# Turning a chunk's normalised rows last in its step, in the first 4-head layer of a four-block attention kernel

## What is computed

```python
def _layer_norm(x, g, b):
    mean = jnp.mean(x, axis=-1, keepdims=True)
    std = jnp.std(x, axis=-1, keepdims=True, ddof=1)
    return g * (x - mean) / (std + EPS) + b
def _mha_layer(q, k, v, Wq, bq, Wk, bk, Wv, bv, gamma, beta):
    ...
    attn = jax.nn.softmax(scores, axis=-1)
    ...
    out = jnp.einsum('hbqk,hbkd->hbqd', attn, Vh)
    out = out.transpose(1, 2, 0, 3).reshape(B, Sq, d)
    out = out + q
    return _layer_norm(out, gamma, beta)
...
for i in range(L):
    enc = _mha_layer(q, k, v, Wq[i], bq[i], Wk[i], bk[i], Wv[i], bv[i], gamma[i], beta[i])
    enc = jax.nn.leaky_relu(enc @ Wff[i] + bff[i], negative_slope=0.2) + enc
    q, k, v = (enc, enc, enc)
```

## Time and profile before

| | us |
|---|---|
| median of 3 runs (lowest, highest) | 1656.14 (1652.9, 1657.09) |
| the profiled execution | 1650.79 |
| its span | 1649.0 |
| PE busy | 1377.1 (84%) |
| DVE busy | 1053.1 (64%) |
| ACT busy | 757.9 (46%) |
| POOL busy | 523.9 (32%) |

### The profile page before, as it was taken

One profiled execution on the slowest core, in us unless ns is written; L12 is line 12 of the kernel. 1 busy time (PEld: TensorE's weight loads), 2 busy tenths in 40 slices (PEclk: granted clock), 3 DMA queues, 4 the chain that ended last, 5 costly groups with the idle time before them and its releaser, 6 DMA issues.

```text
span 1649.0 us, 22006 instructions
## 1 busy us (share of the span) xinstructions
PE 1377.1 (84%) x7498; PEld 795.2 (48%) x7498; DVE 1053.1 (64%) x2640; ACT 757.9 (46%) x1062; POOL 523.9 (32%) x330
## 2 busy tenths in 40 slices
PE   5878999999759978788999869799997668588896
PEld 3423333333348856543444346444443557444796
DVE  5677777777265357756566458676563877675754
ACT  5304555555767444532333435233334534254664
POOL 4000000000231033215777842178876436101222
PEclk8958999999969999998999979799997889899998
DMA  6853333330000000364312306713400020640001
GB/s 233 218 143 55 55 55 55 56 55 2 26 1 1 1 1 32 115 198 90 87 44 52 106 1 185 206 44 90 91 26 26 1 33 1 155 81 3 1 1 51
DMA packets 79850, 110.32 MB, mean 67 GB/s; under 512 B 16576, under 2 KB 55674, under 8 KB 77946
## 3 DMA queue, kind: packets, MB, share of 16 engines
q1 hardware_dynamic: 79737, 108.91, 26.6%
HBM read 70.55 MB, written 37.80 MB: 66 GB/s over the span
## 4 chain that ended last, share of the span: by engine, by line
PE 36%; DVE 22%; POOLq 19%; issue 9%; ACT 6%; DVEq 3%; DMA 2%; POOL 1%; SPq 1%; ACTq 0%
POOLq L1057 19%; PE banks L1145 5%; PE banks L1459 5%; PE banks L1444 4%; PE banks L1088 4%; PE banks L2007 3%; PE banks L1121 3%; DVE max_parts L1282 3%; DVE mask_rows L1278 2%; DVE scratch L1278 2%; PE banks L1099 1%; PE banks L2033 1%; PE banks L2023 1%; DVE max_parts L1267 1%; ACT x_feat L1245 1%
## 5 line engine op out<-in xcount | busy, mean ns | idle before, releaser
L1245 ACT ACTIVATE x_feat<-banks,key_bias 128x1024 f32<-128x1024 f32 x160 | 176.4, 1113 | 271.6 <-PE banks L1130 210.2
L1056 POOL TENSOR_TENSOR x_feat<-x_feat 128x1024 f32<-128x1024 f32 x112 | 269.3, 2405 | 75.1 <-ACT x_feat L1245 63.2
L1088 PE MATMUL banks<-stacks 128*128 128x512 f32 (+4 forms) x640 | 229.2, 405 | 30.0 <-DVE max_parts L1271 9.2
L1145 PE MATMUL banks<-x_feat,v_group 128*64 128x512 f32 (+4 forms) x1312 | 232.1, 568 | 10.9 <-ACT x_feat L1245 10.3
L1245 ACT ACTIVATE x_feat<-banks 128x1024 f32<-128x1024 f32 (+3 forms) x224 | 179.5, 839 | 125.5 <-PE banks L1124 84.5
L1088 PEld LDWEIGHTS banks<-stacks 96*128 96x128 bf16 (+1 forms) x640 | 77.4, 138 | 200.0 <-DVE max_parts L1271 87.8
L1414 POOL TENSOR_TENSOR stacks<-w_even,stacks 128x512 fp32r<-128x512 f32 x16 | 21.9, 1396 | 463.1 <-ACT stacks L1406 463.1
L1121 PE MATMUL banks<-stacks 99*128 99x512 bf16 (+3 forms) x512 | 139.5, 347 | 11.4 <-DMA stacks<-neg_max_parts 6.7
L1271 DVE CUSTOM_DVE_ANT_0 scratch<-banks,mask_rows 128x512 f32<-128x512 f32 x128 | 88.2, 689 | 54.6 <-PE banks L1088 54.6
L1129 PE MATMUL banks<-stacks 128*128 128x512 f32 x256 | 111.2, 434 | 9.5 <-DMA stacks<-neg_max_parts_r 9.5
L1444 PE MATMUL banks<-stacks 128*128 128x512 f32 x384 | 102.5, 406 | 8.2 <-DVE stacks L1426 4.0
(11 more groups left out here) (286 smaller groups left out, 2570.3 us busy)
## 6 DMA issues: line engine op xcount, KB each, us to landing
stacks<-q_parts_r SPq DMA_DIRECT2D x18, 512.0 KB, 12.2
stacks<-k_parts_r SPq DMA_DIRECT2D x18, 512.0 KB, 14.2
q_parts_r<-stacks SPq DMA_DIRECT2D x16, 512.0 KB, 2.8
k_parts_r<-stacks SPq DMA_DIRECT2D x16, 512.0 KB, 3.6
v_group<-v SPq DMA_DIRECT2D x14, 512.0 KB, 14.7
stacks<-q_parts SPq DMA_DIRECT2D x16, 384.0 KB, 5.2
w_even<-in_w SPq DMA_DIRECT2D x4, 1024.0 KB, 6.7
stacks<-q_parts SPq DMA_DIRECT2D x16, 256.0 KB, 5.4
```

Of the source, the lines that this page charges most:

```text
L1056: e.tensor_tensor(total, total, p, ALU.add)
L1088: m = e.matmul(PS[:, bank, at:at + wide], q[0:rows, h, qt * P:(qt + 1) * P], keys[0:rows, h, k0:k0 + wide], start=True, stop=True, skip_gr ...
L1145: m = e.matmul(PS[w * h:w * (h + 1), bank, t.q0:CH], V[:, h, :], PB[:, t.index % 2, h // 2, h % 2, 0:CH - t.q0], start=t.first, stop=t.las ...
L1245: e.activation(dst, PS[:, 2 * (st % 2):2 * (st % 2) + 2, 0:CH - t.q0], ACT.Exp, scale=A.scale, bias=bias).then_inc(s.p_ready, 1)
```

## The change

In the first layer alone (`front`), three things move. On PE, the turn of `y_tok` goes from behind the scores to the end of step i = 2. On PE again, the first half of the feed-forward goes in step i = 3 from ahead of the mask's turn and of `turn_weights` to behind them. On ACT, the copies of the turned `y_tok` go from the head of step i = 2 to its end.

```diff
@@ layer_tensor
-            if i == 2 and ok(-1):
+            if i == 2 and not front and ok(-1):
                 e.wait_ge(nm.normed, c)
                 turn("y", c - 1, Y3)
-            if i == 3 and ok(-1):
+            if i == 3 and not front and ok(-1):
                 forward(c - 1, 0)
...
             if front and 0 < t <= NT:
                 turn_weights(t - 1)
+            if i == 3 and front and ok(-1):
+                forward(c - 1, 0)
...
             if front and 0 < t <= NT:
                 with_values(t - 1)
+            if i == 2 and front and ok(-1):
+                e.wait_ge(nm.normed, c)
+                turn("y", c - 1, Y3)
@@ layer_scalar
-            if i == 2 and ok(-1):
+            if i == 2 and not front and ok(-1):
                 take("y", c - 1, (COLS["gamma"] + 2 * l, COLS["beta"] + 2 * l))
...
             if i > 1 and ok(-2):
                 take_projected(c - 2, i - 2)
+            if i == 2 and front and ok(-1):
+                take("y", c - 1, (COLS["gamma"] + 2 * l, COLS["beta"] + 2 * l))
```

## The result

The changed kernel took 1642.91 us (median of 8 runs, 1636.98 to 1649.01) against 1655.49 us before (8 runs). The ratio is 0.9927, with a 95% interval of 0.9902 to 0.9953: faster by 12.1 us, interval 7.8 to 16.2. Timed again later beside other kernels, the same kernel gave 0.9954 (0.9931 to 0.9977). The 9.8 us forecast lie in both intervals. Taken off the median that the forecast started from, the first ratio gives 1656.14 x 0.9927 = 1644.0, at the fast end of the range of 1643 to 1652.

The account below looks back on a forecast made before the run. No engine is full; PE waits 14.2 us in four chunks of the first 4-head layer for normalised rows. Filling them gives 1.9 + 3.3 + 2.7 + 1.9 = 9.8 us off 1656.14: 1646.3, range 1643 to 1652.

Parts of the forecast that it names:

- Chunk 0: First 512 tokens of the first 4-head layer: scores of tile 7 start earlier, gain 1.9 us, 1.0 at half clock.
- Chunk 1: Second 512 tokens: feed-forward starts at 644.0 instead of 647.30, gain 3.3 us, 2.1 with the half clock left.
- The 1.6 us of clock: Chunk 1's eight query and projection matmuls: 1.6 us come back if the half clock came from the wait before.
- Chunk 2: Third 512 tokens: scores of tile 15 start at 676.3 instead of 679.00, gain 2.7 us, bounds 2.1 and 3.1.
- Chunk 3: Last 512 tokens, no scores left: feed-forward starts at 706.1 instead of 708.04, gain 1.9 us, bounds 1.7 and 2.1.
- Behind 708 us the stage is PE and DVE back to back and shifts whole: From chunk 3's feed-forward to the stage's end: everything moves earlier together, so the gain is not hidden.
- B: PE waits instead for ACT's weights copy, 2.2 us behind the normalise: only 4.8 us gained, 1651.3; chance 0.14.
- C: Stage's end: the next attention's loads land no earlier and are waited for, gain given back, 1656; chance 0.05.
- D: Slower: `y` turned and copied later delays the mask's turn and feed-forward, 1662 with 1.5 us each; chance 0.05.
- the prediction's estimate of 7.5 us: Sum if a table-load drain preceded each weights copy: about 2.3 us lower, 1.4 at chunk 0, 0.9 at chunk 2.

Follow-up runs that it names:

- the run with chunks 0 to 2: The change applied to chunks 0 to 2 only, chunk 3 keeping the old order: stage 165.41 us against 170.54 before, ratio 0.9941.
- the small matmuls in the kernel before: Kernel before, order untouched, with 52, 30, 60 and 76 unused constant matmuls ahead of the `y_tok` turns: stage 166.81 us against 170.54, ratio 0.9966.
- the second trace: The changed kernel run once more, unaltered: stage 161.76 us against 162.72 in the first trace, ratio to before 0.9954.
- turn only: Against before, only the turn of `y_tok` and its copies move, the feed-forward keeping its old place: stage 164.30 us, ratio 0.9966.
- beta late: The change, with DVE adding beta behind subtraction and value in chunk 3: stage 159.37 us against the change's 162.72, ratio to before 0.9945.
- the small matmuls in chunk 3 alone: The change plus 24, 10 and 40 unused constant matmuls in chunk 3's PE waits: stage 160.83 us against the change's 162.72, ratio to before 0.9904.

## Why the prediction came out right, step by step

**The sum.** 9.8 us forecast, 7.8 and 8.8 in two traces of the stage (8.8 and 9.0 by the chunks), 12.1 (7.8 to 16.2) and 7.6 (3.8 to 11.4) in the times. Mechanism and sign were right, the single terms were not all. In part the nearness of the sum is luck: 1.3 us that the forecast priced at nothing (the feed-forward's own move) stand against 1.4 to 2.6 us that chunk 3 did not give.

**Chunk 0,** 1.9 forecast: 1.80 and 1.81. Where the stage's first 32 us differ (32.81 against 31.80), a half clock met other matmuls ahead of the change's first instruction.

**Chunk 1,** 3.3 forecast: 4.12 and 3.07. The 1.6 us of clock came back in one trace and partly in the other, in the run with chunks 0 to 2 not at all. That the half clock came from the wait before it is borne out by the small matmuls in the kernel before: 3.60 us in place of 5.19. It may not be the only wait that does it: in the second trace and in the run with chunks 0 to 2 the matmuls met a half clock with no wait for `y_tok` ahead of them, in a stretch that begins within 2 us of the 2.54 us that PE waits for GpSimd's weights in step 9. The feed-forward's start came 3.5 us earlier against the normalise (7.65, before 11.18), forecast 3.3; the rest of 4.12 is its own move.

**Chunk 2,** 2.7 forecast: 3.57 in both. The scores of tile 15 start 2.7 us earlier against the normalise, as said (671.18 - 664.94 = 6.24, before 679.00 - 670.04 = 8.96), and 3.0 in the second trace, at full clock, where the forecast had 3.1. The missing term is the feed-forward's own move, which the forecast priced at nothing: with the turn in place it fills PE's waits of 0.88 and 0.57 us for the value bank, worth 0.74 in chunk 2 and 0.59 in chunk 1 (turn only against the change).

**Chunk 3,** 1.9 forecast: -0.66 and +0.51. Here a step failed. The feed-forward does start 1.8 us earlier against the normalise (7.03 us, before 8.86), by the very chain forecast: ACT's early copy, DVE's wait for GpSimd, beta, subtraction, value. But "Behind 708 us the stage is PE and DVE back to back and shifts whole" left out that PE has less to do in front of it and sits idle for 2.5 us, behind which the feed-forward and projection run at half clock: 2.7 us more for these two in the first trace, 1.6 in the second. With small matmuls in the waits this loss is gone, with beta late the loss and part of the wait. The term itself was also too large: the 1.8 us hold against a kernel before whose turn and projection ran in part at half clock (1.97 and 2.46 us in chunk 3); with small matmuls in the waits of both orders the new one is 0.7 us ahead.

**The rivals.** B (the wait moves to ACT) holds in chunk 0, as the forecast had it, and in part in chunk 2 once the clock is full: 1.12 us ahead of L2059 in the second trace. C (given back at the end) did not come: from the second half of chunk 3's feed-forward to the row DMAs it takes 33.95 us before (714.51 to 748.46) and 33.95 with the change (706.50 to 740.45). D did not come: the feed-forward waits for the copies of `y_tok` nowhere in the change, 0.4 us in one chunk if only the turn is moved; the mask's turn waits for them once, 0.7 us in chunk 3 of the second trace, where PE then waits for DVE anyway. The drain that the Trainium skill, page "ScalarE: Activation LUTs", section "What ACT_TABLE_LOAD costs", adds to a table load is not in these traces either (the exponential starts 613.93 - 612.64 - 1.28 = 0.01 us behind it), so the prediction's estimate of 7.5 us from that page has no support here, near as it is to the first stage's 7.8.

**Order and clock apart.** Before with its waits filled by matmuls that compute nothing: -3.7 us, the clock's part. The change then adds the order's: in chunks 0 to 2, 25.95 + 32.59 + 28.49 = 87.03 against 79.97, 7.1 us. That the throttled state is the default and activity releases it is what the Trainium skill, page "TensorE: Matmul & The Clock Gate", section "What's actually happening", states; the run of before with small matmuls agrees (mean granted clock of the stage 0.95 against 0.90).

**What stays open.** The first timing of the change shows 4 us more than its stage, the second 1 us less; over the twelve timed kernels the ratios show on average some 2 us more gain than the stages and 1 us more than the chunks, the small matmuls in chunk 3 alone 6 and 4. Whether the later stages, which no edit touches, gain a little or the draws were lucky can't be told: their length ranges from 896.9 to 914.4 us in these traces.

## What to carry to other kernels

Where one queue serves a pipeline of steps, put the instruction that waits for the longest chain last in its step, and check on each other engine that its partner (here ACT's copies) moves too, else the order deadlocks (by the code; it was not run) or the exponential's chain stays behind it. Count what really lies between old and new place: the move is worth as much as the work that stands there, and where there is none (chunk 3) it mostly moves the idle time. A wait of PE can cost twice, once as a wait and once as slow matmuls behind it, so a gain taken from a wait in one place may be lost to the clock at the next; matmuls of constants into a free bank are a cheap test of which it is. Where the draw of the clock moves a stage by as much as an edit does, compare it piece by piece from one landmark to the next, and leave out the pieces that the edit cannot reach.

## What the runs showed of the hardware that was not expected

One program's execution differs from the next by where the half clock falls: the same 3777 matmuls behind the stage took 900.75 us at a mean granted clock of 0.93 and 914.42 us at 0.91. Stage lengths, by contrast, repeat to 0.01 us per chunk where the clock agrees (26.40 and 26.41, 29.14 and 29.14, before and with chunk 3 alone changed).

GpSimd's multiply of 128 x 308 took 0.70 us beside small instructions of DVE and 1.60 us (1.60, 1.61, 1.61 in chunks 0 to 2) where it started while DVE added beta, in the changed kernel's timelines of POOL and DVE:

```profile
609.79 0.70 POOL L2331 TENSOR_TENSOR o_feat<-o_feat,recip 128x308 f32<-128x308 f32 x1 [2.34 <-DVE recip L2226]
...
615.53 1.60 POOL L2331 TENSOR_TENSOR scratch<-scratch,recip 128x308 f32<-128x308 f32 x1 [0.49 <-DVE recip L2226]
```

```profile
615.36 1.22 DVE L423 TENSOR_TENSOR x_res<-x_res,rows_odd 128x1024 f32<-128x1024 f32 x1
```

It goes the other way too. With beta late, DVE's subtraction, 0.69 us at most other places, took 1.80 where it started during GpSimd's multiply by gamma, and ended 0.6 us behind it:

```profile
691.21 2.35 POOL L2372 TENSOR_TENSOR x_res<-y_tok,rows_odd 128x1024 f32<-128x1024 f32 x1 [5.64 <-ACT y_tok L453]
```

```profile
692.32 1.80 DVE L2257 TENSOR_TENSOR stacks<-w_even,stacks 128x512 fp32r<-128x512 f32 x1 [2.54 <-ACT stacks L2147]
```

A drop of the clock need not come right behind a wait, nor each time: 2.09 us of waiting before chunk 1's turn were followed by full clock for the turn (1.10 us) and only then by the half, and the same 0.55 us before chunk 3's turn of the change by half clock in one trace (1.77 us) and full in the other (1.09).
